# Moving the transposes of x one group ahead in a fused attention block, with g_in folded into the weights

## The reference

```python
xn = layernorm(x, g_in)                       # over the 512 features, times g_in
q = (xn @ Wq).reshape(b, n, H, DH) * DH**-0.5 # Wq 512 x 1024
k, v = split(xn @ Wkv)                        # Wkv 512 x 128, one k and v for all heads
k, v = concat([null_k, k]), concat([null_v, v])
sim = einsum('bhid,bjd->bhij', q, k) + concat([null_bias, attn_bias])
sim = causal and key mask (sim)
out = softmax(sim) @ v                        # heads side by side, 128 x 1024
return x + layernorm(out @ Wo, g_out)
```

## Time and profile before

| | us |
|---|---|
| median of 3 runs | 1152.41 |
| the runs | 1154.45, 1152.06, 1152.41 |
| span of the profiled execution (its own time) | 1154.5 |
| PE busy | 1061.4 (92%) |
| PEld busy | 923.9 (80%) |
| POOL busy | 804.2 (70%) |
| DVE busy | 729.0 (63%) |
| ACT busy | 674.2 (58%) |

### The profile page before, as it was taken

How to read it: one execution, slowest core, us unless ns; L and a number is a source line. 1 busy time by engine, 2 the same in 40 slices (tenths; PEclk the granted TensorE clock), 3 DMA queues, 4 the chain that set the end, 5 groups by cost and what they waited for, 6 DMA issues and landing times.

```text
span 1154.5 us, 43028 instructions
## 1 busy us (share of the span) xinstructions
PE 1061.4 (92%) x14464; PEld 923.9 (80%) x14464; DVE 729.0 (63%) x3536; ACT 674.2 (58%) x2666; POOL 804.2 (70%) x1488
## 2 busy tenths in 40 slices
PE   4799999999999999999999999999999999999975
PEld 4678888888888888888888888888888888888864
DVE  4757666656666666766765766755766665666551
ACT  3656556566556556556655655656655656655651
POOL 2657777667777667777767777767777766777763
PEclk9999999999999999999999999999999999999987
DMA  8211211211221211220221121121121121121011
GB/s 224 64 40 49 67 57 40 66 61 45 68 65 31 67 60 47 66 67 31 65 66 44 65 66 41 55 66 56 50 68 51 45 67 58 48 66 47 30 39 36
DMA packets 51548, 67.72 MB, mean 59 GB/s; under 512 B 13888, under 2 KB 25664, under 8 KB 51392
## 3 DMA queue, kind: packets, MB, share of 16 engines
q1 hardware_dynamic: 49280, 63.21, 17.6%
q10 hardware_dynamic: 2112, 2.10, 0.6%
HBM read 40.11 MB, written 16.78 MB: 49 GB/s over the span
## 4 chain that ended last, share of the span: by engine, by line
PE 77%; ACT 8%; issue 6%; DVE 4%; POOL 1%; ACTq 0%; DVEq 0%; POOLq 0%
PE ps_pv L424 33%; PE ps_proj L430 32%; PE ps_s L387 7%; PE ps_pv L411 4%; ACT exp_bot L679 3%; ACT exp_top L679 2%; DVE o_lo L513 2%; ACT xt_hi L710 1%; DVE logit_bot L492 1%; PE ps_proj L448 1%; ACT o_hi L687 1%; ACTq L221 0%; DVEq L221 0%; DVE y_stats L521 0%; DVEq L225 0%
## 5 line engine op out<-in xcount | busy, mean ns | idle before, releaser
L679 ACT ACTIVATE exp_bot<-logit_bot,neg_max 128x129 f32<-128x129 f32 x512 | 201.7, 397 | 342.3 <-DVE neg_max L492 336.9
L430 PE MATMUL ps_proj<-xt_hi,wq_hi 128*128 128x256 f32 x1024 | 298.5, 292 | 4.1 <-DVE q_sb L568 3.9
L790 POOL TENSOR_TENSOR bias_b<-bias_c,mask_add 128x256 f32<-128x256 f32 (+1 forms) x512 | 289.6, 598 | 1.6 <-DVE neg_max L492 0.3
L492 DVE CUSTOM_DVE_ANT_0 logit_bot<-ps_s,bias_b 128x128 f32<-128x128 f32 x512 | 128.7, 289 | 255.4 <-PE ps_s L387 226.8
L430 PE MATMUL ps_proj<-xt_lo,wq_hi 128*128 128x256 f32 x1024 | 288.0, 281 | 0.0
L430 PE MATMUL ps_proj<-xt_hi,wq_lo 128*128 128x256 f32 x1024 | 287.9, 281 | 0.0
L424 PE MATMUL ps_pv<-wo_hi,o_hi 128*128 128x512 f32 x512 | 211.8, 414 | 51.1 <-DVE o_lo L513 51.1
L799 POOL TENSOR_TENSOR w_nrm<-exp_bot,w_inv 128x256 f32<-128x256 f32 x256 | 156.6, 612 | 120.0 <-DVE w_inv L501 118.8
L424 PE MATMUL ps_pv<-wo_lo,o_hi 128*128 128x512 f32 x512 | 204.9, 400 | 0.0
L424 PE MATMUL ps_pv<-wo_hi,o_lo 128*128 128x512 f32 x512 | 204.8, 400 | 0.0
L430 PEld LDWEIGHTS ps_proj<-xt_hi,wq_hi 128*128 128x128 f32 x1024 | 192.8, 188 | 14.3 <-issue 5.1
(11 more groups left out here) (61 smaller groups left out, 1850.7 us busy)
## 6 DMA issues: line engine op xcount, KB each, us to landing
x_in<-in_x_dram SPq DMA_DIRECT2D x32, 512.0 KB, 4.1
x_res<-in_x_dram SPq DMA_DIRECT2D x64, 256.0 KB, 2.8
out_dram<-y_out SPq DMA_DIRECT2D x64, 256.0 KB, 2.0
v_rep<-v_raw SPq DMA_DIRECT2D x256, 32.0 KB, 1.9
w_raw<-in_L_cond_Wq_dram ACTq DMA_DIRECT2D x4, 512.0 KB, 7.9
w_raw<-in_L_cond_Wo_dram SPq DMA_DIRECT2D x4, 512.0 KB, 6.1
mask_u<-in_mask_BxS_bk_dram SPq DMA_DIRECT2D x32, 32.0 KB, 3.7
bias_c<-in_fside_16xSxS_dram SPq DMA_DIRECT2D x4, 128.0 KB, 8.1
```

The costliest lines, as they stand in the source:

```text
L430: mm = pe.matmul(ps[:, 0:TOK], w[:, k, cols], xt[:, k], start=(j == 0), stop=(j == len(todo) - 1))
L492: ins = nc.vector.tensor_tensor_reduce(out_[:, e, 0:keys_], ps_s[e][:, from_:from_ + keys_], bias[:, e], -1.0, 0.0, ALU.add, ALU.min, neg_ ...
L679: ins = nc.scalar.activation(out_[:, s, j], in_[:, s, j], ACT.Exp, bias=neg_max[:, s, k:k + 1], scale=-1.0, accum_out=w_sum[:, s, k:k + 1])
L790: ins = nc.gpsimd.tensor_tensor(out_, bias, key_mask, ALU.add)
```

## The change

Four things change together.

- x0 and x1 are transposed in step 5, two groups ahead of the group that is running, just before q2 and q3 of the next group; step 1 keeps q7 alone. `xt_hi` and `xt_lo` get two buffers. The two banks go on in turn, so that q2 follows x0 in its bank and q3 follows x1, and their waits are written anew. The x tiles of group 1 are still made in step 1 of group 0.
- The statistics of x move from steps 4 and 5 to step 1 on VectorE, the root from step 5 to step 2 on GpSimd (there ahead of `normalize`), the normalised x from step 7 to step 3 on ScalarE. `x_in` gets two buffers, and its loads wait for the normalised x of a group earlier. The load for the odd groups goes in front of a store; the load for the even groups stays where it was.
- g_in is multiplied into Wq and Wkv when their high and low parts are made at the start, in four pieces for each former one. So x0 and x1 are taken out of their banks without g_in, in one 512-wide operation for each tile and engine: a copy for the high part and a tensor_tensor subtraction for the low part.
- At the start x_rstd(1) on GpSimd comes before the causal selection of the bias, the statistics of group 1 before the third piece of Wq's low part, and the normalised x of group 0 before Wkv's high part.

```diff
 FRONT = {
     0: [("q", 5, 0), ("q", 6, 0)],
-    1: [("q", 7, 0), ("x", 0, 1), ("x", 1, 1)],
+    1: [("q", 7, 0)],
     2: [("kv", 0, 1)],
     4: [("q", 0, 1), ("q", 1, 1)],
-    5: [("q", 2, 1), ("q", 3, 1)],
+    5: [("x", 0, 2), ("x", 1, 2), ("q", 2, 1), ("q", 3, 1)],
     6: [("q", 4, 1)],
 }
-STEP_STATS, STEP_XN, STEP_V, STEP_MASK = 4, 7, 7, 7
+STEP_STATS, STEP_RSTD, STEP_XN, STEP_V, STEP_MASK = 1, 2, 3, 7, 7
...
-        x_in = sb("x_in", [P, GB, DIM])
+        x_in = sb("x_in", [P, 2, GB, DIM])
...
+        def bank_of(f, slot, kind, i):
+            if kind == "x":
+                return ps_proj[(slot + i) % 2]
+            return ps_proj[(slot + place_in_frame(f, kind, i)) % 2]
...
             def load_x_and_mask(q, k):
-                sp.wait_ge(xn_made, GB * (2 * q + k))
+                sp.wait_ge(xn_made, GB * (2 * q + k - 1))
...
                 spread_v(2 * p + 1)
+                if not last:
+                    load_x_and_mask(p + 1, 1)
                 if not first:
                     store(p, -1, True)
-                if not last:
-                    load_x_and_mask(p + 1, 1)
...
                 if kind == "x":
+                    if isinstance(f, int) and f < 2:
+                        wait(pe, q_made, QT * f - XT + i + 1)
+                    else:
+                        wait(pe, q_made, QT * (f - 1) + i + 1)
                     if i == 0:
                         wait(pe, xn_made, GB * (f + 1))
...
+                    elif i in (2, 3) and not start and not alone:
+                        wait(pe, xt_lo_made, XT * (f + 1) + i - 1)
...
+            def x_low(f, slot, i):
+                x_raw, hi, lo = halves_of(f, slot, i)
+                wait(dve, xt_hi_made, XT * f + i + 1)
+                nc.vector.tensor_tensor(lo, x_raw, hi.bitcast(F32), ALU.subtract).then_inc(xt_lo_made, 1)
...
+            def x_high(f, slot, i):
+                x_raw, hi, lo = halves_of(f, slot, i)
+                wait(act, proj_done, proj_count(f, "x", i))
+                nc.scalar.copy(hi, x_raw).then_inc(xt_hi_made, 1)
...
-                nc.vector.tensor_tensor(wq_piece(wq_lo, i), raw_piece(i, KT), wq_piece(wq_hi, i).bitcast(F32),
-                                        ALU.subtract).then_inc(wq_lo_made, 1)
+                for k in range(KT):
+                    nc.vector.scalar_tensor_tensor(
+                        out=wq_piece(wq_lo, i)[:, k], in0=raw_piece(i, KT)[:, k], scalar=gin_col[:, k:k + 1],
+                        in1=wq_piece(wq_hi, i)[:, k].bitcast(F32), op0=ALU.mult,
+                        op1=ALU.subtract).then_inc(wq_lo_made, 1)
...
+            x_rstd_of(1)
+            pool.wait_ge(x_shift_made, 2)
             pool.wait_ge(bias_shifted, 2)
             causal_bias()
             masked_bias(0, 0, 0)
             masked_bias(1, 0, 1)
-            x_rstd_of(1)
```

More of the change, by code:

```diff
@@ L60 @@
 }
[L61 to L64, removed]
-STEP_STATS, STEP_XN, STEP_V, STEP_MASK = 4, 7, 7, 7
+PARTS = [("kv", 0)] + [("q", i) for i in range(QT)]
+USES = len(PARTS) + XT
+PROLOGUE = [("x", 0), ("x", 1)] + PARTS[:PARTS.index(("q", 4))]
+STEP_STATS, STEP_RSTD, STEP_XN, STEP_V, STEP_MASK = 1, 2, 3, 7, 7
 ITEMS = (
@@ L169, in attention_block @@
         ld_bias = sem("ld_bias")
-        ld_x = sem("ld_x")
+        ld_x = [sem(f"ld_x{i}") for i in range(2)]
         ld_v = sem("ld_v")
@@ L260, in front_parts @@
             for kind, i, ahead in table.get(t % CG, ()):
-                if last and t // CG + ahead == 2:
+                if last and t // CG + ahead >= 2:
                     continue
@@ L555, in front @@
             def front(f, slot, kind, i):
-                use = USE[kind, i]
-                ps = ps_proj[(use + slot) % 2]
                 if kind == "x":
[L559 to L565, removed]
+                    x_low(f, slot, i)
                 elif kind == "q":
-                    wait(dve, proj_done, USES * f + use + 1)
-                    nc.vector.tensor_copy(q_sb[:, slot, i // 2, i % 2], ps[:, 0:TOK]).then_inc(q_made, 1)
+                    wait(dve, proj_done, proj_count(f, kind, i))
+                    nc.vector.tensor_copy(q_sb[:, slot, i // 2, i % 2], bank_of(f, slot, kind, i)[:, 0:TOK]).then_inc(q_made, 1)
             nc.vector.memset(eps_col[:], EPS)
@@ L723, in _ @@
                 act.dma_start(raw_piece(i, KT), wq_piece(wq.rearrange("(k p) n -> p k n", p=P), i)).then_inc(ld_wq[i], 16)
+            x_norm(0, 0)
+            act.wait_ge(ld_cols, 16 * COL_LOADS)
             act.wait_ge(ld_wkv, 16)
-            nc.scalar.copy(wkv_hi[:].rearrange("p k n -> p (k n)"), wkv_raw).then_inc(wkv_hi_made, 1)
-            x_norm(0)
-            act.wait_ge(ld_cols, 16 * COL_LOADS)
+            for k in range(KT):
+                nc.scalar.activation(wkv_hi[:, k], wkv_raw[:, 2 * DH * k:2 * DH * (k + 1)], ACT.Copy,
+                                     scale=gin_col[:, k:k + 1]).then_inc(wkv_hi_made, 1)
             act.wait_ge(filled, 1)
@@ L731, in wq_high @@
                 act.wait_ge(ld_wq[i], 16)
-                nc.scalar.copy(wq_piece(wq_hi, i), raw_piece(i, KT)).then_inc(wq_hi_made, 1)
+                for k in range(KT):
+                    nc.scalar.activation(wq_piece(wq_hi, i)[:, k], raw_piece(i, KT)[:, k], ACT.Copy,
+                                         scale=gin_col[:, k:k + 1]).then_inc(wq_hi_made, 1)
             def wo_high(i):
@@ L774, in body @@
                         first_extras[t]()
-                    if not last and t % CG == STEP_XN:
-                        x_norm(2 * p + t // CG + 2)
+                    if not last and t < CP:
+                        if t % CG == STEP_XN:
+                            x_norm(2 * p + t // CG + 2, t // CG)
             run_pairs(act, body)
```

108 lines of the change are left out of this document (62 added, 46 removed).

## The result

The changed kernel takes 1200.66 us (median of 4 runs, 1199.74 to 1202.21), the kernel before 1153.28 in the same comparison (4 runs, 1152.06 to 1154.45): 1.0404 times as long, 95% interval 1.0383 to 1.0425. The profiled execution has a span of 1198.7 us, 44.2 more than before; the medians are 47.4 apart. Predicted were 1195 (1165 to 1214) and "slower". The prediction was right, and for its own reason, though two of its terms stand in another place or size than it said.

The account below looks back on a forecast made before the run. The prediction took TensorE's issued work plus its gaps as the bound: +1.20 us a group for 29 groups (+34.8), loads +5.6, group 30 -2.7, start +5, in sum +42.7 on 1152.4, giving 1195 us (range 1165 to 1214).

Parts of the forecast that it names:

- Step 1, -1.19: TensorE in step 1: without the eight transposes, scores(2) follow the last Q tile after 0.08 us, not 1.27; -1.19 a group.
- step 3, -0.58: Output projection of step 3: starts 4.86 to 5.06 us after scores(2), not 5.54; -0.58 a group, gap left about 0.96.
- Step 5, +2.97: Step 5: q2 waits for x0 to leave its bank, starting 6.76 us after scores(4), not 3.79; +2.97 a group.
- The rule on VectorE and GpSimd: x_low stays at 0.69 us beside GpSimd, having one PSUM input; if held up like the 4.58 row, up to 3.4 later.
- Loads, +5.6: Even groups' x loads land late for the statistics, delaying logits(2) by about 0.4 us in 14 groups; +5.6, bounds 0 and 13.
- Start, +5: Kernel start: more weight pieces and a causal selection about 3 us later, partly absorbed by idle time; +5, bounds -2 and +11.
- group 30, -2.7: Last group, with neither transposes nor statistics: -1.19 - 1.45 = -2.7 us.
- (a): Step 5: ScalarE serves x_high(0) as soon as the transposes end; +0.46 a group, whole +21, 1174 us; chance 0.09.
- (b): Step 5: x_high and x_low hidden behind the second transposes; -0.49 a group, 1135 to 1146 us; chance 0.10.
- (c): More is late: even loads, x_low(0) held up by GpSimd, or granted clock falling in new gaps; +63, 1215 us; chance 0.09.
- (d): Step 3's gap closes wholly as statistics do not delay logits(2), loads harmless; -29, 1161 us; chance 0.06.
- the last step: From profiled span to median time: the profiled span of 1154.5 lies 2.0 above the median, so 1152.4 + 42.7 = 1195 us.

Follow-up runs that it names:

- experiment 9: Experiment 2 with the first half of scores(0) and scores(2), which reads two Q tiles alone, ahead of the wait for the last copy: 1146.37 us.
- Experiment 10: Experiment 2 with x's statistics at the end of step 2, the root behind normalize(3) and the normalised x in step 5: 1131.14 us.
- experiment 2: The changed kernel with the eight x transposes in the middle of step 7's output projection and both takings at the end of step 7: 1144.86 us.
- experiment 3: The changed kernel with step 5 in the order x0, q2, x1, q3: 1169.48 us.
- experiment 4: The changed kernel with the y_nrm of step 4 behind the x halves of step 5 on ScalarE: 1187.96 us.
- experiment 5: The changed kernel with the load of x for even groups ahead of the last store of the pair: 1196.36 us.
- experiment 7: Experiment 2 with x's statistics in step 3, the root in step 4 ahead of normalize(4) and the normalised x in step 6: 1152.65 us.
- experiment 8: Experiment 7 with kv in step 1, q0 in step 2, q1 and q2 in step 4, q3 in step 5: 1192.57 us.
- experiment 6: Experiment 2 with x's statistics in step 3, the root in step 4 and the normalised x in step 5: 1165.47 us.
- experiment 11: Experiment 10 with the edit of experiment 9 as well: 1128.55 us.
- experiment 12: Experiment 2 without the folding, g_in multiplied at the takings again in four 256-wide operations on each engine: 1142.92 us.

## Why the prediction was right, step by step

- **Step 1, -1.19, and step 3, -0.58.** Together -1.77 predicted, -1.62 measured (-0.52 and -1.10). The remaining wait was predicted at 0.96 and is 0.61 + 0.35 = 0.96. Its place was wrong: I let scores(2) start 0.08 us after the last Q tile, as if the copy of that tile weren't needed, and put the whole wait before the output. Scores(2) need the copy; TensorE stops there for 0.61 and again for 0.35. The sum comes out because, as I had it, VectorE's row of work between the copy and logits(2) sets the time and not TensorE, which experiment 9 shows: moving 0.35 us of scores ahead changed only where the idle time stands. Experiment 10 shows that the statistics are what makes that row late: without them there the output's wait is gone.
- **Step 5, +2.97.** Measured +2.72 to q2. The chain is the predicted one: y_nrm at +4.48, as forecast, x_high at +5.16, as forecast. The mis-sized term is x_high(0): priced 0.78 as y_nrm, released after 0.61 (x_low starts at 5.77, predicted 6.00). x_low: priced 0.69, two take 1.29. Experiments 2 and 3 take away all of the bank wait and most of it, and get 56 and 31 us back; experiment 4 takes y_nrm out and gets 12.7.
- **The rule on VectorE and GpSimd.** The first x_low took 0.69 us with masked_bias beside it on GpSimd all the time (487.25 to 489.50), the pair 1.29, where the bound from the row of 4.58 would have been far above. The Trainium skill (SBUF — State Buffer, "Who interferes with whom") has a vector operation with at most one SBUF input undisturbed, except in 2-port modes, which by the same section a tensor_tensor doesn't have; the trace agrees. That rival to the price is refuted.
- **Loads, +5.6.** 4.3 by experiment 5, 3.6 by its trace. The mechanism is right, but only five such waits are seen (0.24 to 0.79 us), not 14.
- **Start, +5; group 30, -2.7.** Scores(0) of group 1 start at 73.00 and not at 66.26: +6.7. The sum for the start named weight pieces and the causal selection and left out the clock. TensorE works 12.7 us at a granted clock of 0.5 there (in 28.9 to 35.7 and 52.8 to 63.0), and 3.4 before; half of the difference, 4.7 us, is my estimate of the clock's part. That the +5 came near is therefore luck in part. The loop's mean period is 35.73 (28 periods between the transposes at 92.99 and 1093.45), 1.36 over before, for 29 groups +39.4, where 34.8 + 5.6 = 40.4 was predicted. 44.2 - 6.7 - 39.4 leaves -1.9 for the end, and group 30 is 1.96 shorter than before (32.40 against 34.36): -2.7 had left out that scores(2) still wait 0.61 for q7's copy.
- **From the span to the time.** The spans differ by 44.2 where the sum said 42.7. The other 4 of the 5.7 us between 1195 and 1200.66 are the last step: it took 2.0 off for the profiled execution, while the time of the changed kernel's is 1.8 above its span (1200.46 against 1198.7).
- **Rivals.** (a) would need x_high at once: it starts behind y_nrm. (b), the sign: the idle time before q2 is 1.39, far over its point of 0.2 to 0.5. (c): the clock stayed at 1.00 in the loop; it was lower in the start alone. (d) fell with the 0.96 that stayed.

So the 44 us are: bank wait in step 5 about +1.6 a group beyond the moved transposes, which experiments 2 and 3 tie to it; less 0.35 won before step 3's output, together 1.21 for 29 groups, 35 us; and some 9 us of loads (4), start (7) and end (-2). The idea of the edit, taking the x halves out of step 1 and getting the statistics of a group early, is sound. Put where the bank isn't wanted (experiment 2) and with the statistics behind logits(2) (experiment 10) it is worth 2.1% (1.9 to 2.4).

## What to carry to other kernels

When work that writes a shared PSUM bank is moved, look at who wants that bank next and how much of TensorE's own work lies between: here 0.6 us lay before a taking by two engines in turn that needs 1.3 (0.61 + 0.69) and was queued behind a norm, and 3.0 us of an unrelated product hid it wholly. A wait that is merely shifted is recognised when two idle times on the bound engine add up to the old one; the engine to relieve is then the one whose row of work spans both. And an engine's idle time is usable only at the place in its queue where the wait stands: with the 1.5 us of small operations behind normalize(3) no new wait appeared (experiment 10), with them ahead of normalize(4) the new wait of 0.60 to 0.69 was longer than the saved one of 0.36 (experiment 7). Last, look at the granted clock of every stretch before a loss is put down to a wait alone: waits of 1.4 us a group left it at 1.00 here, waits of 2.0 us were followed by 0.5 in 12 groups (experiment 8), and in the start it hid behind what looked like slow weights.

## What the runs showed that I had not expected

- ScalarE's 512-wide copy out of PSUM without scale and bias stands in the trace as CAST and takes 0.59 us (two in 1.06), where the 512-wide activation with scale and bias takes 0.78.
- In all experiments with the transposes in step 7 (2 and 6 to 12) TensorE idles 0.25 to 0.9 us with "issue" before every second scores(0), once in a turn of the loop: 13 times, 5.8 to 8.2 us in all. The kernel before and the changed one have no such gap there. What it waits for the profile doesn't show, and it wasn't tried.
- Four GpSimd operations on 128x2 elements that depend on each other take 1.5 us (501.24 to 502.73); the power alone is 0.70.
